# Seven PSUM banks in one pool, given out by the plan, in place of a ring of four and a ring of three

## The reference, cut to what matters

```
h = layernorm(x) * (1 + ca) + sa
x = x + ga * attention(h)        # layer 0: causal, with ALiBi; layer 1: causal, with rotary embedding
h = layernorm(x) * (1 + cb) + sb
x = x + gb * feed_forward(h)     # layer 0: gated, with token shift; layer 1: one linear map
```

## Time and profile before

| | us |
|---|---|
| median of the 3 runs | 2794.85 |
| lowest and highest | 2792.37, 2794.88 |
| the profiled execution | 2790.14 |
| its span, first to last instruction | 2788.4 |

### The profile page before, as it was taken

How to read it: one execution, slowest core, us unless ns; L and a number is a source line. 1 busy time by engine, 2 the same in 40 slices (tenths; PEclk the granted TensorE clock), 3 DMA queues, 4 the chain that set the end, 5 groups by cost and what they waited for, 6 DMA issues and landing times.

```text
span 2788.4 us, 55137 instructions
## 1 busy us (share of the span) xinstructions
PE 2464.7 (88%) x18968; PEld 1027.6 (37%) x18968; DVE 2156.4 (77%) x6588; ACT 1711.5 (61%) x3458; POOL 1025.8 (37%) x1558
## 2 busy tenths in 40 slices
PE   6898888988999999988999989999999989897686
PEld 4323333423334343343434333443433434333223
DVE  3897758788887988878887988878888788872961
ACT  3475575555765667756675666656677566664264
POOL 4222542244242443335243442434433352335222
PEclk9999999999999999999999999999999999998788
DMA  6510143121413222311423214131223114004000
GB/s 213 171 58 20 37 130 99 34 80 48 139 48 101 62 89 83 111 49 50 122 67 93 77 53 139 54 104 51 88 83 111 49 50 136 21 29 136 30 2 16
DMA packets 142394, 218.29 MB, mean 78 GB/s; under 512 B 21190, under 2 KB 62556, under 8 KB 142052
## 3 DMA queue, kind: packets, MB, share of 16 engines
q1 hardware_dynamic: 142120, 214.77, 25.5%
HBM read 137.87 MB, written 77.89 MB: 77 GB/s over the span
## 4 chain that ended last, share of the span: by engine, by line
PE 54%; DVE 24%; ACT 10%; issue 5%; POOL 5%; DMA 1%; SPq 0%; DVEq 0%; POOLq 0%; ACTq 0%
PE ctx_ps L1649 11%; PE big L1630 11%; PE big L1567 10%; DVE small L1398 8%; PE big L1556 8%; PE small L1608 7%; ACT probs L1184 6%; DVE mx L1396 4%; PE big L1681 4%; ACT xn L1233 4%; DVE stats L1352 3%; PE big L1664 2%; DVE region L1461 2%; DVE mx L1398 1%; DVE region L1499 1%
## 5 line engine op out<-in xcount | busy, mean ns | idle before, releaser
L1184 ACT ACTIVATE probs<-big 128x512 f32<-128x512 f32 (+2 forms) x2560 | 1221.4, 563 | 429.9 <-PE big L1630 421.4
L1398 DVE CUSTOM_DVE_ANT_0 small<-small,mask 128x128 f32<-128x128 f32 (+3 forms) x2048 | 942.9, 520 | 141.6 <-PE small L1608 130.7
L1630 PE MATMUL big<-stack_q,stack_k 64*128 64x512 f16 (+3 forms) x6144 | 711.8, 330 | 81.1 <-ACT probs L1184 52.8
L1396 DVE TENSOR_REDUCE mx<-small 128x1 f32<-128x512 f32 x1024 | 652.1, 682 | 102.8 <-PE small L1608 96.5
L1649 PE MATMUL ctx_ps<-probs,v_ones 128*17 128x512 f32 (+3 forms) x6144 | 646.6, 498 | 28.8 <-POOL probs L1063 19.3
L1063 POOL TENSOR_SCALAR_AFFINE_SELECT probs<-probs 128x512 f32<-128x512 f32 x512 | 329.0, 653 | 674.4 <-ACT probs L1184 674.1
L1608 PE MATMUL small<-stack_k,stack_q 64*128 64x512 f16 (+3 forms) x3072 | 458.0, 335 | 130.9 <-DVE mx L1398 76.0
L1630 PEld LDWEIGHTS big<-stack_q,stack_k 64*128 64x128 f16 x6144 | 232.0, 95 | 610.5 <-issue 356.5
L1608 PEld LDWEIGHTS small<-stack_k,stack_q 64*128 64x128 f16 x3072 | 128.9, 94 | 549.6 <-DVE mx L1398 248.7
L1398 DVE DVE_READ_ACCUMULATOR2_ANT mx<- 128x1 f32 x2048 | 286.2, 140 | 0.0
L1556 PE MATMUL big<-hT,w_qkv 128*128 128x512 f32 x512 | 274.3, 640 | 1.5 <-ACT probs L1184 1.4
(11 more groups left out here) (94 smaller groups left out, 1938.6 us busy)
## 6 DMA issues: line engine op xcount, KB each, us to landing
image<-region SPq DMA_DIRECT2D x192, 256.0 KB
stack_q<-image SPq DMA_DIRECT2D x64, 512.0 KB, 3.8
stack_k<-image SPq DMA_DIRECT2D x64, 512.0 KB, 4.7
lo_dram<-region SPq DMA_DIRECT2D x64, 256.0 KB
w_qkv<-wqkv SPq DMA_DIRECT2D x16, 768.0 KB, 6.4
x_res<-x SPq DMA_DIRECT2D x32, 256.0 KB, 3.5
stack_q<-lo_dram SPq DMA_DIRECT2D x128, 64.0 KB, 4.2
stack_k<-lo_dram SPq DMA_DIRECT2D x128, 64.0 KB, 5.2
```

The lines of the kernel that those rows point to most:

```text
L1184: s.activation(probs[:, n % HELD, heads, q0:], big[:, at.slot(turn), 0:len(pairs) * width] .rearrange("p (h q) -> p h q", h=len(pairs)), A ...
L1396: last = v.reduce_max(to, held, AX)
L1398: last = v.tensor_tensor_reduce(out=held, in0=held, in1=mask[:, BANK - width:], scale=1.0, scalar=3.0 * NEG, op0=ALU.add, op1=ALU.max, acc ...
L1630: last = te.matmul(big[:, at.slot(at.turn() + parity), j * width:(j + 1) * width], stack_k[rows, c, g * PAIR_N + pair, kt * P:(kt + 1) * P ...
```

## The change

The two tensors become one, `big`, with `BANKS` = 7, and which bank an item gets is decided in `plan`: `Model.take_bank` picks the bank that the model expects to be free first, of all seven, whoever had it before. `MOST` limits a use to 5 banks at a time for turns and 4 for maxima. Only at the start, while three of the banks hold the one-off products, turns keep to the other four. The list of banks goes into the program (`slot`, `uses`, `max_bank`), so each item waits on the semaphore of its own bank, for that bank's use number. Before a `max` step TensorE therefore waits on two semaphores in place of one, and before a `join` VectorE waits on one for each bank that the group used. A turn may now wait for VectorE's reduction of a bank, and a `max` step for ScalarE.

Three numbers of the planner change along with it (in `QK_LAGS`, `SEEN` and `FEED`), and a table `PHASES` is added to `AHEAD`. The arithmetic, the number of instructions on the engines and their shapes stay the same; the order changes throughout.

```diff
-RING = 4
-SMALL = 3
+BANKS = 7
+ONCE_BANKS = 3
+MOST = {"turn": 5, "max": 4}
...
+GROUP_STEPS = 2 * PAIR_N * len(MAX_BANKS)
...
-QK_LAGS = (0.0, 0.7758, 0.9862, 2.7516, 5.9576)
+QK_LAGS = (0.0, 0.7758, 0.9862, 2.3391, 5.9576)
...
-SEEN, DMA_NS = 232.7037, 466.9094
+SEEN, DMA_NS = 326.2839, 466.9094
...
-FEED = {"DVE": 0.0215, "ACT": 0.1761}
+FEED = {"DVE": 0.0215, "ACT": 0.1346}
...
+    def open_to(self, use):
+
+        return range(BANKS if self.taken["max"] else BANKS - ONCE_BANKS) if use == "turn" else range(BANKS)
+
+    def bank_free(self, use, n=1):
+
+        own, first = self.ends[use], MOST[use] - n + 1
+        return max(sorted(self.banks[b] for b in self.open_to(use))[n - 1], own[-first] if len(own) >= first else 0.0)
+
+    def take_bank(self, use):
+
+        b = min(self.open_to(use), key=lambda b: self.banks[b])
+        self.taken[use].append((b, self.used[b]))
+        self.used[b] += 1
+        self.banks[b] = 1e18
+        return b
+
...
-            return max(own, self.ring[self.turn % RING], self.ring[(self.turn + 1) % RING])
+            return max(own, self.bank_free("turn", 2))
...
-            return max(self.at(("stack", unit, item[2])), self.small[self.step % SMALL], self.small[(self.step + 1) % SMALL])
+            return max(self.at(("stack", unit, item[2])), self.bank_free("max", 2))
...
+            self.opened = self.take_bank("turn")
...
+            ahead = AHEAD[name] + (PHASES[name][phase] if name in PHASES else 0.0)
+            return cost - PULL[name] * (done * all_[name] - taken[name] + ahead * all_[name] / N_UNITS)
...
-        return (self.turn() if turn is None else turn) % RING
+        return MODEL.taken["turn"][self.turn() if turn is None else turn][0]
...
-        big = ctx.enter_context(nc.psum_tensor("big", [P, RING, BANK], f32))
+        big = ctx.enter_context(nc.psum_tensor("big", [P, BANKS, BANK], f32))
+        small = big[:, BANKS - ONCE_BANKS:]
...
-                        last.then_inc(s_freed, 1)
+                        last.then_inc(freed[at.max_bank(parity)[0]], 1)
...
-                    dve.wait_ge(s_freed, at.now("max", SMALL))
+                    for bank, use in dict(MODEL.taken["max"][:at.own("max")][-GROUP_STEPS:]).items():
+                        dve.wait_ge(freed[bank], use + 2)
...
-                    pe.wait_ge(s_freed, at.now("max", 2))
+                    for parity in range(2):
+                        bank, use = at.max_bank(parity)
+                        pe.wait_ge(freed[bank], use + 1)
```

More of the change, by code:

```diff
@@ L216, in ease @@
     return CHAIN_EASE if engine == "DVE" else EASE
+PHASES = {"max": (-0.0897, 0.0000, 0.0000, 0.0000, 0.0000, 0.0000, 0.0000, 0.0514), "pre": (0.0000, 0.0000, 0.0000, 0.1303, 0.0000, 0.0000, 0.0000, 0.0000), "post": (0.0000, 0.0000, -0.3023, 0.0000, -0.0043, 0.0000, 0.1945, 0.0000)}
 FIRST_FEED, FEED_WAIT = {"max": 216.0, "score": 430.0}, 300.0000
@@ L228, in __init__ @@
         self.free = {"PE": 0.0, "ACT": 0.0, "DVE": 0.0, "POOL": 0.0, "SP": 0.0}
-        self.ring, self.small, self.shape = [0.0] * RING, [0.0] * SMALL, None
-        self.turn = self.step = 0
+        self.banks, self.used, self.shape = [0.0] * BANKS, [0] * BANKS, None
+        self.taken, self.ends, self.opened = {"turn": [], "max": []}, {"turn": [], "max": []}, None
         self.ready, self.pipe = {}, 0.0
@@ L252, in needs @@
         if kind == "half":
-            return max(self.needs(item[2]), self.ring[self.turn % RING])
+            return max(self.needs(item[2]), self.bank_free("turn"))
         if kind == "score":
@@ L260, in needs @@
         if kind == "max":
[L261 removed]
+            return max(self.at(("stack", unit, item[2])), self.bank_free("max", 2))
         if kind == "rows":
[L263 removed]
+            return max(self.at(("join", unit, item[2])), self.bank_free("turn"))
         own = {"proj": [("ctx", unit), ("scale", unit)], "turned": [("xn", unit)], "qk": [("h", unit), ("pre_loads", unit)], "value": [("h", unit)],
                "gate": [("mix", unit)], "key": [("mix", unit)], "y": [("h", unit), ("square", unit), ("scale", unit), ("bias", unit, 3)]}[kind]
[L266 removed]
+        bank = 0.0 if item in self.ready else self.bank_free("turn")
         return max(self.at(*own), bank)
@@ L334, in bank @@
     def bank(self, end):
-        self.ring[self.turn % RING] = end
-        self.turn += 1
+        b = self.take_bank("turn") if self.opened is None else self.opened
+        self.opened, self.banks[b] = None, end
+        self.ends["turn"].append(end)
     def play(self, item):
@@ L364, in play @@
                 cost = sum(piece_width(qt, blk) * 1.04 + 75 for qt, blk, _ in item[4])
-                self.small[self.step % SMALL] = self.run("DVE", end + SEEN, cost)
-                self.step += 1
+                b = self.take_bank("max")
+                self.banks[b] = self.run("DVE", end + SEEN, cost)
+                self.ends["max"].append(self.banks[b])
         elif kind == "rows":
@@ L685, in slot, with max_bank @@
     def slot(self, turn=None):
-        return (self.turn() if turn is None else turn) % RING
+        return MODEL.taken["turn"][self.turn() if turn is None else turn][0]
     def uses(self, turn):
-        return turn // RING
-    def small(self, parity):
-        return (self.own("max") + parity) % SMALL
+        return MODEL.taken["turn"][turn][1]
+    def max_bank(self, parity):
+        return MODEL.taken["max"][self.own("max") + parity]
     def done(self, item):
@@ L1263, in _ @@
                 dve.sem_inc(bank, 1)
-            dve.sem_inc(s_freed, SMALL)
             dve.sem_inc(pv_done, HELD)
```

10 lines of the change are left out of this document (4 added, 6 removed).

## The result

| | before | after |
|---|---|---|
| median of the runs, us | 2793.61 (4 runs) | 2704.61 (4 runs) |
| ratio, 95% interval | | 0.968 (0.967 to 0.970) |
| span of the profiled execution, us | 2788.4 | 2701.1 |

The change makes the kernel faster by 89 us, 3.2%. I had forecast 2755 us, 40 us less. The direction was right; the gain is more than double the forecast and falls just outside the range (2705 to 2802), where I had put the rival "more than the sum" (2703 us, 13%).

What follows compares the result with a forecast made beforehand. TensorE's work was taken to set the end, with its idle time in the even stretch mostly waits for banks. Maxima 40 plus changes of shape 10 less 10 coming back made 40 us off 2794.85: 2755 us, range 2705 to 2802.

Steps and rivals of the forecast that it cites:

- more than the sum: Rival: TensorE and VectorE stop waiting for each other, 115 us of bank waits less a fifth, 92 us off, 2703 us; 13%.
- the planner's numbers: New lags and phases move pre and post work against the maxima; 0, with 23 us to either side.
- What bounds the kernel: TensorE's work mostly sets the end; 144 of 216 us idle in the even stretch (100 to 2500 us) are bank waits.
- Maxima, 40 us: Maxima products in the even stretch: more TensorE work between a bank's filling and reuse shortens 87.4 us of waits by 40.
- Turns, 0 us: Banks of the turns, scores among them: distances hardly change, so 0 off 57 us of waits, 25 us to either side.
- coupling: Rival: scores stand behind late VectorE reductions they never depended on before; slower, near 2810 us; 12%.
- Changes of shape, 10 us: On TensorE's array, 103 fewer changes between shapes at 0.1 us of lost overlap each give 10 us; bounds 0 and 20.
- The clock: TensorE's granted clock, 0.98 in the even stretch: fewer gaps could return up to 48 us; named only for a rival.
- The wait instruction, 0 us: A second semaphore wait at each of 1152 maxima steps, 51 ns each, is hidden by TensorE's sequencer; 0, at most 59 us.
- What comes back, 10 us: As TensorE advances, VectorE's share rises to 83.5% and its longer jobs hit earlier; a fifth, 10 us, given back.

Runs made afterwards that it cites:

- common rotation: All seven banks handed out in one strict rotation to both uses: 2897.3 us in the order of the kernel before, 2877.0 us in the changed kernel's order.
- The two rings with the new numbers: The kernel before, rings of four and three banks kept, given the planner's changed QK_LAGS, SEEN and FEED and the PHASES table: 2864.9 us.
- three neighbours of the changed kernel: The changed kernel with only SEEN shifted from 326.3 ns to 306.7, 316.5 or 336.1 ns: 2761.8, 2759.5 and 2771.1 us.
- the neighbour at 316.5 ns: The changed kernel with SEEN at 316.5 in place of 326.3 ns, a shift of 3%: 2759.5 us, ratio to before 0.988.

## Why the prediction was wrong

The step that failed is the term for the planner's numbers, which I put at 0 and bounded by 23 us; with the pool the runs show 101 us for them together, and with the two rings they cost 72 us. In the terms of the profile, I forecast 30 us less idle time (40 less 10 that come back) and 10 us less busy time, and measured 54.7 and 32.6 us.

*What bounds the kernel.* Right. The gain came out of the even stretch, the last part stayed as it was (289 and 286 us), and TensorE's waits for banks fell.

*Maxima, 40 us.* Right in size: waits of this product for all readers fell from 87.4 to 42 us in the even stretch, those for VectorE alone to 32.3 us, a little under the 35 to 60 that I had named. The mechanism was only half right. I argued from more TensorE work between filling and reuse; with a common rotation there is as much of it, and the kernel is slower than before. It also has to be the right reader's bank.

*Turns, 0 us.* The waits of the score product for banks were about as forecast (about 53 us against 46 before), with VectorE's reductions in them, 32.2 us, just past the 30 us at which I had called myself wrong on coupling. Coupling exists and was paid for by 26.6 us less of waiting for the exponentials. With the other turns, above all the transposes (12.3 us for ScalarE's exponentials before, 0.6 after), the waits for banks of turns fell from 61.5 to 55 us.

*Changes of shape, 10 us.* The busy time of TensorE fell by 32.6 us, more than three times the 10 us. Up to 22 of them go with the time at the half clock, which leaves 10.6 us or more: near the 10 us, but that may be chance. Other runs do not bear the term out. The two rings with the new numbers have 2062 changes of shape, 168 fewer than before, and TensorE is busy for 2487.9 us, 23 more, at a clock of 0.939. The changed kernel's own order, with the same 2127 changes, is busy for 2476.8 us with the common rotation (clock 0.945) and 2493.0 us on the two rings (0.954), against 2432.1 us. So TensorE's busy time moves by tens of us where the changes of shape stay the same.

*The clock.* In the sum I gave it nothing and only named it for a rival. That term was mis-sized: up to 22 us of busy time. The mean clock was 0.98 in the even stretch before and after, a row too coarse to see it in; the half level fell from about 217 to 173 us in the whole execution. Of these 44 us, 27 lie in the even stretch (up to 14 us of busy time) and 17 in the last part, where VectorE's share is 91% for 100 us and little came of them. The Trainium skill's section on bank cycling (TensorE: Matmul & The Clock Gate, A second HAM failure mode: psum-queue depth-cycling) ties small pauses between groups of products to lost clock. The trace agrees in direction: 54.7 us less idle time went with 44 us less at the half level. Which of the two causes the other is not shown.

*The wait instruction, 0 us.* Wrong: 1152 of them cost 18 us in the kernel before, about a third of 51 ns each. I read from one place in the timeline that they are hidden. The sign that I had named, idle time that only TensorE's own issue ends, does not catch it: that is 0.6 us in the even stretch after and 1.0 before. Where the 18 us arise is open: in the profile they are about half idle time and half busy time.

*The planner's numbers, 0 us.* **This is the step that failed.** I bounded them by 23 us, half of the true data waits, as if they only moved a few items. Runs show 83 us for the phases table alone and 101 us for all of them, and a shift of one of them by 3% is worth 55 to 66 us. I had priced the pool and the plan apart. The pool at ordinary plans brings about 63 us and the better draw about 26. My 2755 is close to the three neighbours of the changed kernel (2760 to 2771), and that is luck: I took it from the actual two orders, and the same count gives the neighbour at 316.5 ns the same distances.

*The rival "more than the sum".* Its 2703 us are almost the measured time, and that is luck as well. It wanted 115 us of bank waits gone and 23 given back; in the even stretch 46 us went from the maxima and 6 from the turns, and about 8 came back at true data. The rest of the gain is the shorter busy time, gaps too short to be listed as waits (5 us) and 6 us less idle time in the last part.

*What comes back, 10 us.* In size right: true data waits rose from 46.7 to about 55 us (20.6 + 16.9 + 12.8 + 3.7 and smaller ones), at the join and the normed input. I named VectorE's load as the cause; its idle time before maxima rose from 199 to 247 us where I had expected 160, so its mean load was not what stood in the way.

What makes this one plan better than its neighbours stays open. The first waits of the neighbour at 316.5 ns, over the whole execution, and its clock:

```profile
PE big L1634 <- DVE mx L1421: 48.9, 85, 3.7
PE big L1690 <- ACT xn L1257: 35.1, 13, 9.4
...
PE big L1656 <- ACT probs L1208: 27.4, 58, 2.0
...
PE big L1634 <- DVE mx L1419: 22.3, 39, 2.0
```

```profile
core 0: 2758.0 us, clock 0.959
```

It waits longer for maxima banks (71.2 us, where the changed kernel has 56.2 over the whole execution) and for the exponentials (27.4 and 15.5), and has more time at the half clock (0.959 and 0.968). Of the 57 us by which its span is longer, 29 are busy time of TensorE and 28 idle time. These go together, and no run singles one out.

## What to carry to other kernels

Buffers in one pool, each given to whoever the plan expects to need it next, beat the same number in fixed rotations (52 us here with the order untouched), but only if the choice follows the predicted end of the reader; a plain common rotation was worse than two separate ones under the old order (2897 against 2793 us). Where a planner with tuned numbers orders the work, price the structure over several neighbouring settings before and after: one pair of runs mixes the structure with the luck of the draw, here about 63 and 26 us. And a wait instruction that is implied by another may be left out; over a thousand of them cost 15 to 18 us in the kernel before.

## What the runs showed of the hardware

TensorE's additional wait instructions read 51 ns each on its sequencer; 1152 more of them cost 16 ns each and 1394 fewer gave 11 ns each, in the kernel before. In the changed kernel 1138 fewer gave about 4 ns each, which its runs can hardly tell from nothing.

The same 18968 matrix instructions of TensorE were busy for 2432.1 us in the changed kernel and for 2493.0 us in its own order on two rings, where 592 us were idle (269 in the changed kernel). In the changed kernel and its three neighbours the busy time is least where the mean clock is highest: 2461.2 us at 0.959, 2442.5 at 0.963, 2445.6 at 0.964, 2432.1 at 0.968.
